# An attention and gated-FFN kernel on one core: the last group of heads in two halves of queries, half of its projection ahead and half in fp32, and the transposes of o behind the second maxima

## The reference, cut to what matters

```python
x = L0_attn_x                                   # (8, 512, 256): 8 rows of 512 tokens
xn = layernorm(x)
# attention: 16 heads of 16, scale 1/4
qkv = xn @ qkv_w + qkv_b
attn = softmax(einsum('bnhd,bmhd->bhnm', q, k) * scale)
out  = einsum('bhnm,bmhd->bnhd', attn, v).reshape(b, n, c)
attention = out @ proj_w + proj_b
# FFN: hidden 768, weights are integers / 127
h = silu(xn @ wg.T) * (xn @ wu.T)
x = x + attention + h @ wd.T
```

## Time and profile before

| | |
|---|---|
| median of 3 runs | 630.44 us (628.84 to 630.52) |
| the profiled execution, in all | 631.72 us |
| its span | 629.8 us |
| TensorE busy | 605.6 us (96%) |
| VectorE busy | 490.8 us (78%) |
| ScalarE busy | 373.6 us (59%) |
| GpSimd busy | 172.4 us (27%) |

### The profile page before, as it was taken

How to read it: one execution, slowest core, us unless ns; L and a number is a source line. 1 busy time by engine, 2 the same in 40 slices (tenths; PEclk the granted TensorE clock), 3 DMA queues, 4 the chain that set the end, 5 groups by cost and what they waited for, 6 DMA issues and landing times.

```text
span 629.8 us, 10979 instructions
## 1 busy us (share of the span) xinstructions
PE 605.6 (96%) x3616; PEld 329.5 (52%) x3616; DVE 490.8 (78%) x647; ACT 373.6 (59%) x483; POOL 172.4 (27%) x181
## 2 busy tenths in 40 slices
PE   7898999999999999999999999999999999999885
PEld 6654455554645555554545545455555455554434
DVE  5897887788887887888887887878878777878712
ACT  3545665666566565675566564766557655666571
POOL 3215144220621225220532215221252202222210
PEclk9999999999999999999999999999999999999998
DMA  8770181114612184203812166012822037221101
GB/s 277 230 120 3 68 234 52 53 36 163 157 36 50 59 245 82 51 4 130 202 50 51 34 180 162 12 50 93 230 64 51 3 124 180 51 51 36 35 2 36
DMA packets 38204, 58.98 MB, mean 94 GB/s; under 512 B 6048, under 2 KB 21280, under 8 KB 38176
## 3 DMA queue, kind: packets, MB, share of 16 engines
q1 hardware_dynamic: 38176, 58.61, 34.3%
HBM read 37.10 MB, written 20.97 MB: 92 GB/s over the span
## 4 chain that ended last, share of the span: by engine, by line
PE 85%; DVE 6%; ACT 4%; issue 3%; DMA 1%; POOL 1%; SPq 0%; ACTq 0%; DVEq 0%; POOLq 0%
PE dense L910 36%; PE o_bank L900 19%; PE st_bank L869 16%; PE s_bank L886 11%; DVE neg_max L681 3%; ACT probs L562 2%; DMA probs<-in_L_attn_qkv_w 1%; PE dense L924 1%; PE dense L941 1%; DVE o_blocks L742 1%; ACT qk_parts L578 1%; POOL xn L489 1%; PE s_bank L869 0%; PE dense L968 0%; DVE w_gl L733 0%
## 5 line engine op out<-in xcount | busy, mean ns | idle before, releaser
L562 ACT ACTIVATE probs<-st_bank 128x1024 f32<-128x1024 f32 x250 | 255.9, 1024 | 211.0 <-PE st_bank L869 206.7
L681 DVE TENSOR_REDUCE neg_max<-s_bank 128x2 f32<-128x1024 f32 x250 | 304.8, 1219 | 75.8 <-PE s_bank L886 75.0
L900 PE MATMUL o_bank<-probs,v_ones 128*32 128x512 f32 x1024 | 137.2, 608 | 3.8 <-ACT probs L562 3.8
L869 PE MATMUL st_bank<-q_stack,k_stack 50*128 50x512 f32 x500 | 124.7, 495 | 4.4 <-ACT probs L562 4.2
L497 POOL TENSOR_TENSOR hid_tl<-hid,hid_th 128x512 fp32r<-128x512 f32 x48 | 61.7, 1285 | 194.1 <-ACT hid_th L627 194.1
L886 PE MATMUL s_bank<-k_stack,q_stack 48*128 48x512 f32 x500 | 111.6, 442 | 1.2 <-DVE neg_max L681 0.2
L869 PEld LDWEIGHTS st_bank<-q_stack,k_stack 50*128 50x128 f32 x500 | 46.6, 183 | 119.7 <-ACT probs L562 82.5
L886 PEld LDWEIGHTS s_bank<-k_stack,q_stack 48*128 48x128 f32 x500 | 46.9, 184 | 28.9 <-DVE neg_max L681 26.9
L530 POOL TENSOR_TENSOR resid<-resid,p_bias 128x256 f32<-128x256 f32 x32 | 22.5, 736 | 108.9 <-DMA resid<-in_L_attn_x 108.9
L900 PEld LDWEIGHTS o_bank<-probs,v_ones 128*32 128x32 f32 x1024 | 20.2, 108 | 47.9 <-issue 42.6
L709 DVE SCALAR_TENSOR_TENSOR gated<-gated,dense 128x512 f32<-128x512 f32 x48 | 32.7, 681 | 13.2 <-ACT gated L601 11.9
(11 more groups left out here) (104 smaller groups left out, 686.3 us busy)
## 6 DMA issues: line engine op xcount, KB each, us to landing
q_spread<-qk_parts SPq DMA_DIRECT2D x16, 512.0 KB, 3.3
k_spread<-qk_parts SPq DMA_DIRECT2D x16, 512.0 KB, 3.7
q_stack<-q_spread SPq DMA_DIRECT2D x64, 128.0 KB, 3.1
k_stack<-k_spread SPq DMA_DIRECT2D x64, 128.0 KB, 3.3
q_stack<-q_spread SPq DMA_DIRECT2D x64, 64.0 KB, 3.3
k_stack<-k_spread SPq DMA_DIRECT2D x64, 64.0 KB, 3.3
resid<-in_L_attn_x SPq DMA_DIRECT2D x8, 512.0 KB, 5.3
xn<-in_L_attn_x SPq DMA_DIRECT2D x7, 512.0 KB, 3.5
```

The lines of the kernel that those rows point to most:

```text
L562: nc.scalar.activation(probs[:, s % 2, 2 * half:2 * half + 2, :], transposed_bank(row, s, half)[:, :, :], ACT.Exp, scale=SCALE).then_inc(e ...
L681: nc.vector.tensor_reduce(neg_max[:, g % 2, :, NT * pair + qt], score_bank(row, half)[:, :, :], AX_X, ALU.max, negate=True).then_inc(max_d ...
L869: done = nc.tensor.matmul(transposed_bank(row, s, half)[:, r, :], k_stack[rows, pair, P * kt:P * (kt + 1)], q_stack[rows, pair, :], start= ...
L900: done = nc.tensor.matmul(o_bank[32 * j:32 * (j + 1), :], v_ones[:, kt, 8 * (g // 2) + 2 * j + g % 2, :], probs[:, (s - 1) % 2, j, :], sta ...
```

## The change

Seven edits:

- `LEAVE` goes from 1 to 2: the transpose of o stands behind the second maxima of the step, in all rows.
- The chunk "down 0" moves from step 8, slot 2, to step 9, slot 0.
- On ScalarE, `hidden_highs` of slot 1 stand behind that slot's takes.
- In `after_scores` steps (row 7, steps 10 to 15) the second half of `pairs` goes ahead of `probs_v`.
- The projection is no longer a chunk in row 8. `project_first_half` multiplies the first 128 channels for all 4 tiles, three fp32r products each, before the last `probs_v`; the fourth tile uses the free half of `st_bank`.
- The last group's 512 queries are handled in two halves by VectorE alone (`last_group`), and `project_last_half` multiplies `ot` as fp32 with `w_last`, a copy of the lower half of `proj_w` that is loaded early in row 0. `stay_busy` does 6 transposes in place of 24, in the other half of `st_bank`.
- VectorE adds one tile at a time, and the output leaves in three transfers (tiles 0 and 1, tile 2, tile 3).

```diff
--- before.py
+++ after.py
@@ -51,7 +51,7 @@
-BUSY_AFTER = {"last": 24}
+BUSY_AFTER_LAST = 6
@@ -66,8 +66,8 @@
     (7, 0, "q", 1, 1),
-    (8, 0, "k", 1, 1), (8, 2, "down", 0, 0),
-    (9, 2, "down", 1, 0),
+    (8, 0, "k", 1, 1),
+    (9, 0, "down", 0, 0), (9, 2, "down", 1, 0),
     (10, 1, "max", 3, 0), (10, 2, "down", 2, 0),
@@ -108,7 +108,7 @@
-LEAVE, INVERT, DIVIDE, RETURN, HIGH, LOW = 1, 2, 2, 5, 6, 6
+LEAVE, INVERT, DIVIDE, RETURN, HIGH, LOW = 2, 2, 2, 5, 6, 6
@@ -124,7 +124,8 @@
         return FIRST
-    return [c for c in STEADY if 0 <= like + c[4] < ROWS]
+    return [c for c in STEADY if 0 <= like + c[4] < ROWS and not (like == ROWS and c[2] == "proj")]
@@ -228,6 +229,8 @@
+        w_last = raw_d[:, 0:C]
...
@@ -294,6 +305,9 @@
+            if row.like == ROWS:
+                return None
             at = SLOTS * step + slot - delay
@@ -304,6 +318,10 @@
+        def last_bank(t):
+            return (dense[t] if t < DENSE_BANKS else st_bank[:, 0, :])[:, 0:C]
@@ -419,6 +437,9 @@
                     sp.dma_start(p_bias[:, :], proj_b.partition_broadcast(P)).then_inc(bias_in, 16)
+                if row.like == 0:
+                    sp.wait_ge(dense_done, count(Row(-1, -1), ALL, kind="wdown", index=2))
+                    sp.dma_start(w_last, proj_w[P:2 * P]).then_inc(w_last_in, 16)
                 if row.has(0):
@@ -428,11 +449,10 @@
                 if row.like == ROWS:
-                    for half in range(2):
-                        tiles = slice(half * NT // 2, (half + 1) * NT // 2)
-                        sp.wait_ge(dense_free, count(row, ALL, kind="proj", index=half))
+                    for tiles in (slice(0, 2), slice(2, 3), slice(3, 4)):
+                        sp.wait_ge(last_added, tiles.stop)
                         sp.dma_start(out_rows[row.at - 1, :, tiles], resid[:, tiles, :]).then_inc(out_done, 16)
-                    sp.wait_ge(out_done, 16 * (row.at + 1))
+                    sp.wait_ge(out_done, 16 * (row.at + 2))
                 elif row.has(-1):
@@ -530,9 +550,9 @@
                     for slot in range(SLOTS):
-                        if left_at(row, s, slot, DIVIDE) and row.like < ROWS:
+                        if left_at(row, s, slot, DIVIDE):
                             divide(*left_at(row, s, slot, DIVIDE))
-                        if left_at(row, s, slot, LOW, (1, 3)) and row.like < ROWS:
+                        if left_at(row, s, slot, LOW, (1, 3)):
                             attention_low(*left_at(row, s, slot, LOW, (1, 3)))
@@ -642,7 +662,8 @@
                             exp(row, s, slot // 2)
-                        hidden_highs(row, SLOTS * s + slot)
+                        if slot != 1:
+                            hidden_highs(row, SLOTS * s + slot)
                         for chunk in taken_at(row, s, slot):
@@ -652,6 +673,9 @@
                                 square_lows()
+                        if slot == 1:
+                            hidden_highs(row, SLOTS * s + slot)
                         if left_at(row, s, slot, HIGH, (1, 3)):
@@ -745,13 +769,6 @@
-            def divide_last(row, g):
-                dve.wait_ge(inv_done, NG * row.at + g + 1)
-                dve.wait_ge(ot_done, 2 * row.at + g // 2)
-                nc.vector.tensor_tensor(o_norm[:, :, 1, :], o_blocks[:, :, 0:HD],
-                                        inv_sum[:, :].unsqueeze(2).broadcast_to([P, TOK // 32, HD]),
-                                        ALU.mult).then_inc(odd_divided, 1)
@@ -762,22 +779,43 @@
-            def low_last(row):
-                dve.wait_ge(ot_high, 2 * row.at)
-                nc.vector.tensor_tensor(ot_parts[:, 1, 1, :], ot[:, :], ot_parts[:, 1, 0, :].bitcast(F32),
-                                        ALU.subtract).then_inc(ot_low1, 1)
+            def last_group():
+                dve.wait_ge(pv_done, STEPS * ROWS)
+                dve.wait_ge(even_divided, 2 * ROWS)
+                for h in range(2):
+                    blocks = slice(TOK // 64 * h, TOK // 64 * (h + 1))
+                    queries = slice(TOK // 2 * h, TOK // 2 * (h + 1))
+                    nc.vector.transpose(o_blocks[:, blocks, :].rearrange("p b d -> p (b d)"),
+                                        o_bank[:, queries]).then_inc(last_left, 1)
+                    dve.wait_ge(last_left, h + 1)
+                    nc.vector.reciprocal(inv_sum[:, blocks], o_blocks[:, blocks, HD]).then_inc(last_inv, 1)
+                    dve.wait_ge(last_inv, h + 1)
+                    nc.vector.tensor_tensor(o_norm[:, blocks, 1, :], o_blocks[:, blocks, 0:HD],
+                                            inv_sum[:, blocks].unsqueeze(2).broadcast_to([P, TOK // 64, HD]),
+                                            ALU.mult).then_inc(last_divided, 1)
+                    dve.wait_ge(last_divided, h + 1)
+                    if h == 0:
+                        dve.wait_ge(ot_low0, ROWS)
+                    nc.vector.transpose(ot[:, queries], o_norm[:, blocks, :, :].rearrange("p b a d -> p (b a d)")
+                                        ).then_inc(last_ot, 1)
+                dve.wait_ge(dense_free, count(Row(ROWS - 1, ROWS - 1), ALL, kind="down", index=3))
+                for t in range(NT):
+                    dve.wait_ge(last_projected, t + 1)
+                    nc.vector.tensor_tensor(resid[:, t, :], last_bank(t), resid[:, t, :],
+                                            ALU.add).then_inc(last_added, 1)
...
                     invert(*left_at(row, s, slot, INVERT))
-                if row.like == ROWS and left_at(row, s, slot, DIVIDE):
-                    divide_last(*left_at(row, s, slot, DIVIDE))
                 if left_at(row, s, slot, RETURN, (1, 3)):
                     both_return(*left_at(row, s, slot, RETURN, (1, 3)))
-                if row.like == ROWS and left_at(row, s, slot, LOW, (3,)):
-                    low_last(row)
+                if row.like == ROWS and (s, slot) == (0, 0):
+                    last_group()
@@ -974,6 +1012,25 @@
+            def project_first_half():
+                pe.wait_ge(ot_low0, ROWS)
+                for t in range(NT):
+                    if t < DENSE_BANKS:
+                        pe.wait_ge(dense_free, count(Row(ROWS - 1, ROWS - 1), ALL, chunks_of(ROWS - 1)[-1]))
+                    else:
+                        pe.wait_ge(exp_done, 2 * STEPS * ROWS - 1)
+                    for n, (a, b) in enumerate(SPLIT):
+                        nc.tensor.matmul(last_bank(t), ot_parts[:, 0, a, P * t:P * (t + 1)], w_p[b][:, 0, :],
+                                         start=n == 0, stop=False)
+            def project_last_half():
+                pe.wait_ge(w_last_in, 16)
+                for t in range(NT):
+                    pe.wait_ge(last_ot, t // 2 + 1)
+                    nc.tensor.matmul(last_bank(t), ot[:, P * t:P * (t + 1)], w_last[:, :],
+                                     start=False, stop=True).then_inc(last_projected, 1)
@@ -992,13 +1049,11 @@
                 for _ in range(turns):
-                    nc.tensor.transpose(st_bank[:, 0, 0:P], ident[:, :], ident[:, :])
+                    nc.tensor.transpose(st_bank[:, 1, 0:P], ident[:, :], ident[:, :])
...
                     chunk_products(row, chunk, exact)
-                    if row.like == ROWS:
-                        stay_busy(BUSY_AFTER.get(chunk[2:4], 0))
                     if row.like == -1 and chunk[2:4] == ("xn", 1):
@@ -1016,12 +1071,18 @@
                     pairs(row, s, 0)
+                    if after_scores(row, s):
+                        pairs(row, s, 1)
+                    if row.like == ROWS and s == 0:
+                        project_first_half()
                     if 0 < STEPS * row.like + s <= STEPS * ROWS:
...
                         if row.like == ROWS:
-                            stay_busy(BUSY_AFTER["last"])
+                            stay_busy(BUSY_AFTER_LAST)
+                            project_last_half()
                     chunks(row, s, 1, exact)
-                    pairs(row, s, 1)
+                    if not after_scores(row, s):
+                        pairs(row, s, 1)
                     chunks(row, s, 2, exact)
```

More of the change, by code:

```diff
@@ L277, in build @@
         ot_low1 = sem("ot_low1")
+        last_left = sem("last_left")
+        last_inv = sem("last_inv")
+        last_divided = sem("last_divided")
+        last_ot = sem("last_ot")
+        w_last_in = sem("w_last_in")
+        last_projected = sem("last_projected")
+        last_added = sem("last_added")
         dense_done = sem("dense_done")
```

## The result

The changed kernel takes 619.92 us (median of 4, 619.71 to 624.59) against 630.35 for the kernel before beside it (median of 4, 628.84 to 630.52): a ratio of 0.9858, interval 0.9809 to 0.9906. The interval allows any gain from 5.9 to 12.0 us, so the time alone can't tell 9.4 from 10.4; what follows rests on the traces.

The account below looks back on a forecast made before the run. Steady rows were taken as bound by TensorE, the end by a chain of waits. Gains of 4.0 + 2.4 + 3.0 = 9.4 us from a 630.44 us median gave 621.0 us, range 618.5 to 626.0.

Parts of the forecast that it names:

- The steady edits: Waits at steps 9 and 3 of the steady rows go: 2.2 plus 1.8, together 4.0 us, bounds -1 to 4.8.
- the 0.05 us given back: At step 9, second-half scores come within some 0.05 us of waiting for its first maxima; deducted from the gain.
- the slack counted as 0.1 us: Step 9's product overwrites o_bank; the later transpose of o was to end about 0.1 us before the product starts.
- Rival A: The steady waits only move, since VectorE is at 82% and slacks are small: 625.0 us, chance 0.15.
- The cover named for the add: Down 0's add goes behind step 9's first maxima at no cost; without this, up to 0.4 us a row is lost.
- Pairs, projection and clock: Row 7's paired exponentials, projection half ahead, last product at 1.06 us: 2.4 us gain, bounds 1.2 to 3.0.
- the steps counted at no gain: Row 7's steps 10 to 12, said to stay TensorE-bound through their down chunks, so pairing gains nothing there.
- rival B: Low clock stays at the end: TensorE still pauses and the transposes filling the pause are cut; 622.9 us, chance 0.13.
- C: Pairing in the last steps fails, a bank or product still tying them: pace stays 2.61 us, time 623.0, chance 0.08.
- The last group: Two halves on VectorE, 3.1 us, fp32 products at 0.47 a tile: last product to last add 4.65 us, gain 3.0.
- The output transfer: Last add to the span's end, with three transfers instead of two: 4.3 us against 4.26, bounds 3.8 to 4.8.
- Rival D: Slower: products at 31 group ends wait 0.6 us for o_bank behind late transposes of o; 639.6 us, chance 0.04.

Follow-up runs that it names:

- s4_tail: The changed kernel with the three steady edits undone, so only the end is new: 624.09 us, ratio 0.9899 against the kernel before.
- s1_steady: The kernel before with the three steady edits alone (LEAVE, down 0, hidden_highs), old end: 626.64 us, ratio 0.9918.
- s2_leave: The kernel before with only the transposes of o behind the second maxima, down 0 not moved: 631.54 us, ratio 1.0007.
- t2_behind: The changed kernel with the projection's first half behind the last product, replacing the six filler transposes: 619.57 us, ratio 0.9806 against the kernel before.
- t1_unpaired: The changed kernel with the second half of the pairs back behind the product in the last steps: 623.17 us, ratio 0.9865 against the kernel before.
- s3_hidden: The kernel before with only the hidden highs of slot 1 behind the takes, old end: 628.92 us, ratio 0.9957.
- t3_whole: The changed kernel with the last group in one piece on VectorE, products still fp32: 621.75 us, ratio 0.9861 against the kernel before.
- a1_again: The changed kernel once more, unedited: 620.71 us, ratio 0.9849 against the kernel before.
- v1_both: The changed kernel with row 7's down chunks in steps 6 to 9 and the projection's first half behind the last product, no filler transposes: 618.77 us.
- t6_down_early: The changed kernel with row 7's four down chunks in steps 6 to 9 instead of 9 to 11: 619.38 us, ratio 0.9795 against the kernel before.
- t5_no_filler: The changed kernel without the six filler transposes behind the last product: 622.80 us, ratio 0.9874 against the kernel before.

## Why the prediction was right, and where it was off

**The steady edits: right.** The table has 5.02 us where 4.0 stood, but 0.70 of it stands in s4_tail's trace without any steady edit, among it what products at step 10 of rows 0, 4 and 6 seemed to gain. That leaves 4.3, and at full clock the edits are worth 4.1 (s1_steady against before). The gains per place are 0.30 and 0.32: 0.28 was forecast at step 3, and 0.32 at step 9. There the 0.05 us given back came true for another reason than the one named: the second scores do not wait for the first maxima, but the product waits 0.03 to 0.05 us for the transpose of o, so the slack counted as 0.1 us was none. Row 7's step 3, counted as 0.1, gave the full 0.30 and lost it again at step 6. Rival A is out: s1_steady has nearly the whole gain. The cover named for the add was real: s2_leave puts the price of its lack at 0.31 us a row, or all of the gain, close to the bound of 0.4.

**Pairs, projection and clock: right in sum, mis-sized inside.** 2.81 us where 2.4 stood. The pace is 1.98 (said: 1.95 to 2.0), the last product 1.04 us at clock 1.00 (said: 1.06), the projection's open part 1.2 (said: 1.2; t2_behind's 1.22). The start of the last product moved by 2.81 - 0.94 = 1.87 us where the working had 1.5. The miss lies in the steps counted at no gain: on before's scale the product of step 13 starts at 602.39 + 5.02 = 607.41, 0.68 us ahead of 608.09, where the working had 0.14. Steps 10 to 12 were not simply TensorE-bound. The worth of pairing by itself was under-priced more: by the working the unpaired order would have started its last product at 616.35 (the half behind the scores of 614.8), 1.95 us after the paired one, and t1_unpaired starts it 2.82 later. The other 0.94 us is the clock. The last product took 1.98 us at 0.50 in that one execution of before; s3_hidden's trace shows the old end without the loss, and that executions of before at 628.5 to 631.0 lack it too is inferred from their clock of 1.000. The forecast set a sum with that loss in it against a median that held an unknown part of it. At full clock the parts come to some 4.2 + 1.9 + 3.1 = 9.2 us and the time to 9.35, so that 9.4 came out so near is partly luck: the 0.94 us that was not there to win made up for a pairing counted too low. Rivals B and C are out: clock 1.00 through the end, pace 1.98. At 0.999 or more were 14 of 57 executions of before and 6 of 10 of the changed kernel, so the medians' 10.4 us hold some recovered clock. Why the clock holds is less sure than the forecast had it. The last product is at 1.00 in all ten traces with the new end, t1_unpaired's with its pauses among them, and in one of four with the old. And the argument in rival B from the earlier trace rows is weaker than it reads, since the last product itself ran until 617.91, just ahead of the stretch in which the clock came back.

**The last group: right.** 4.53 us where 4.65 stood. The two halves take 2.89 us (610.10 to 612.99, the second shorter than the first), not 3.1; the Trainium skill's formula (VectorE: DVE Perf Modes, "The TRN2 errata"), whose estimate was 2.9, came nearer than my rows. An fp32 tile is 0.54 us, not 0.47: four matmuls in 1.10. But the halves were hardly needed: t3_whole needs 4.80 us and the same time. So 2.8 of the 3.1 us come without them, from the split into high and low taken off the chain and half of the products done ahead; these two were not run apart.

**The output transfer: the term outside its bounds.** It was counted at nothing and gave 0.87 us in the two traces, although one issue of 1.50 us stood in it; 3.39 lies below the lower bound of 3.8. But the 4.26 it was set against is one execution's: s1_steady, with the same old end, has 2.97, s2_leave 4.11 and s3_hidden 4.04, and the changed kernel in a1_again 3.04. How much of the 0.87 is the three transfers' is open. Without the long issue, as in t3_whole, it is 2.5. The low end of the forecast was also added wrongly: all upper ends together give 630.44 - 11.8 = 618.6, so 618.5 holds every one of them and not all but one.

**Rival D** did not occur in its size. Its mechanism is there at one group end of each of rows 0 to 6, where the product waits for the transpose of o, but at 0.03 to 0.05 us and not 0.6.

## What to carry to other kernels

When an engine is busy at 99.8% of a steady stretch, compare the spacing of the same few instructions at each of its places: the two places where it was wider here held some 4 us. Two traces can differ by 0.7 us at one place without the edit in question, so set a gain read from two traces against a third that lacks the edit. A move on a second engine pays only together with the one that makes room for it, so list what stands between the moved instruction and the next one awaited. And put the profiled execution among the others by its clock before a loss seen in it is booked as a gain.

## What the runs showed of the hardware

- TensorE's clock can fall in a stretch where it is busy 4.2 of 5 us: it was 1.00 at 575 to 580 and 0.58 at 580 to 585 in s3_hidden, most of the way down to the level of 1.2 GHz, in steps paced by exponentials. It did not fall in the same steps in the changed kernel's trace, busy 3.82 and 3.35 of 5 us. Moving four dense chunks there left all six of v1_both's runs at full clock, but two of t6_down_early's six still at 0.994.
- At the end a pause of 1.71 us (t5_no_filler) did not lower the clock of the products behind it, so the six transposes were not needed to keep it.
- An issue of an output transfer on SP's queue took 0.36 to 0.46 us, and in nine of the ten traces with the new end one took 1.10 to 1.50, ending 0.36 to 0.40 us behind the end of a 16 KB load of instructions.
- The product waiting for VectorE's transpose of its bank started 0.15 us after the transpose's end, at all eight places where it was the last thing waited for.
- A time outside the span of 2.3 to 2.8 us against 1.75 to 1.95 went with the absence of transposes behind the last product, and in t2_behind took back a part of what the span had gained.
